# Three more products of the last down projection computed by features: a macaron layer on one core

## The reference

```python
x = x + 0.5 * ffn(layernorm(x))
x = x + scan_mixer(layernorm(x))     # z = x W^T, gated scan over time, layernorm
x = x + 0.5 * ffn(layernorm(x))
# ffn: gate = x Wg^T, up = x Wu^T, hidden = silu(gate) * up, out = hidden Wd^T
```

## Time and profile before

| | us |
|---|---|
| median of 3 runs | 1014.11 (1013.87 to 1014.11) |
| the profiled execution's own time | 1013.8 |
| span of its trace | 1012.0 |
| PE busy | 1005.7 |
| DVE busy | 728.7 |
| ACT busy | 438.2 |
| POOL busy | 202.8 |

### The profile page before, as it was taken

The page is one execution under the profiler, slowest core; times in us unless marked ns, Lnnn a source line. Parts: engine busy times, 40 slices in busy tenths (PEclk is TensorE's granted clock), DMA queues, the critical chain, the costliest instruction groups (busy, mean ns, idle before and its releaser), DMA issues.

```text
span 1012.0 us, 13046 instructions
## 1 busy us (share of the span) xinstructions
PE 1005.7 (99%) x4652; PEld 841.6 (83%) x4652; DVE 728.7 (72%) x1070; ACT 438.2 (43%) x711; POOL 202.8 (20%) x243
## 2 busy tenths in 40 slices
PE   8999999999999999999999999999999999999998
PEld 7888888888888888888888888888888888888897
DVE  7755665598988687857978887786587455654693
ACT  6645446456433623223823344232273434332382
POOL 4123343115400200210421020003040222200032
PEclk9999999999999999999999999999999999999999
DMA  6588877769767545746856764554588799874255
GB/s 208 224 312 332 308 255 255 270 211 277 255 223 239 188 158 165 222 139 227 258 181 211 244 221 148 187 159 147 174 277 261 244 328 332 323 239 167 84 187 187
DMA packets 76319, 228.39 MB, mean 226 GB/s; under 512 B 6624, under 2 KB 26080, under 8 KB 68576
## 3 DMA queue, kind: packets, MB, share of 16 engines
q1 hardware_dynamic: 75680, 226.52, 66.1%
q10 hardware_dynamic: 576, 1.05, 0.3%
HBM read 173.02 MB, written 54.53 MB: 225 GB/s over the span
## 4 chain that ended last, share of the span: by engine, by line
PE 99%; DMA 0%; DVE 0%; POOL 0%; ACT 0%; issue 0%; DVEq 0%; ACTq 0%
PE ps_a L1911 8%; PE ps_a L1910 8%; PE ps_a L1912 8%; PE ps_b L1911 7%; PE ps_b L1910 7%; PE ps_b L1912 7%; PE ps_d L1910 7%; PE ps_d L1911 7%; PE ps_d L1912 7%; PE ps_c L1911 6%; PE ps_c L1910 6%; PE ps_c L1912 6%; PE aux L1911 3%; PE aux L1910 3%; PE aux L1912 3%; PE ps_d L2130 1%
## 5 line engine op out<-in xcount | busy, mean ns | idle before, releaser
L1280 DVE TENSOR_TENSOR tmp<-tmp,ps_c 128x512 f32<-128x512 f32 x59 | 40.4, 685 | 119.2 <-PE ps_c L1912 119.2
L1910 PE MATMUL ps_a<-xt,gu 128*128 128x512 f32 x304 | 118.3, 389 | 0.0
L1911 PE MATMUL ps_a<-xt,gu 128*128 128x512 f32 x304 | 118.3, 389 | 0.0
L1912 PE MATMUL ps_a<-xt,gu 128*128 128x512 f32 x304 | 118.3, 389 | 0.0
L1911 PE MATMUL ps_b<-xt,gu 128*128 128x512 f32 x286 | 111.3, 389 | 0.0
L1912 PE MATMUL ps_b<-xt,gu 128*128 128x512 f32 x286 | 111.3, 389 | 0.0
L1910 PE MATMUL ps_b<-xt,gu 128*128 128x512 f32 x286 | 111.3, 389 | 0.0
L1912 PE MATMUL ps_c<-xt,gu 128*128 128x512 f32 x236 | 91.8, 389 | 0.0
L1911 PE MATMUL ps_c<-xt,gu 128*128 128x512 f32 x236 | 91.8, 389 | 0.0
L1910 PE MATMUL ps_c<-xt,gu 128*128 128x512 f32 x236 | 91.8, 389 | 0.0
L1912 PE MATMUL ps_d<-dn,hid 128*128 128x512 f32 (+1 forms) x224 | 83.7, 374 | 0.0
(11 more groups left out here) (290 smaller groups left out, 2324.8 us busy)
## 6 DMA issues: line engine op xcount, KB each, us to landing
dn<-dn_kept SPq DMA_DIRECT2D x92, 512.0 KB, 4.0
gu<-gu_kept SPq DMA_DIRECT2D x46, 1024.0 KB, 5.1
gu<-gu_kept SPq DMA_DIRECT2D x46, 768.0 KB, 5.6
gu_kept<-gu SPq DMA_DIRECT2D x14, 1024.0 KB, 4.5
gu_kept<-gu SPq DMA_DIRECT2D x14, 768.0 KB, 4.2
dn_kept<-dn SPq DMA_DIRECT2D x16, 512.0 KB, 5.1
t_kept<-zx SPq DMA_DIRECT2D x16, 512.0 KB, 4.7
dn<-t_kept SPq DMA_DIRECT2D x16, 512.0 KB, 3.9
```

The lines of the kernel that those rows point to most:

```text
L1280: dve.tensor_tensor(dst, u3s(si), p5_bank(si)[:, :], ALU.add).then_inc(c22_done, 1)
L1910: pe.matmul(dst, a_hi, b_hi, start=start, stop=False, skip_group_check=chained)
L1911: pe.matmul(dst, a_hi, b_lo, start=False, stop=False, skip_group_check=chained)
L1912: return pe.matmul(dst, a_lo, b_hi, start=False, stop=stop, skip_group_check=chained)
```

## The change

P1, Q6 and Q7 go by features too, so only Q4 stays by tokens. The chain in `x_ps` is now copied by ACT after P1 (for result 0), after Q6 (for result 2) and after Q7 (for result 1), and PE waits for these copies (`feature_copied` 2, 4, 6), where it waited for `block_added`. DVE adds P2 to result 0 and Q5 + Q3 to result 2 in feature form (`add_feature`), and for result 1, which is now twice as large (4 rows instead of 2), it adds the two rows of `x_ps` to the two of `z_ps` (`add_third_link`). Q4 gets four banks of its own, one for each unit of tokens, and DVE adds each unit as it is done (`add_unit`). The quadrant copies of result 0 on ACT move from before batch 10's cast to behind batch 14's. The diff, without the semaphores' declarations:

```diff
@@ -64,8 +64,7 @@
               + [(w, i) for w in (Q7, Q3, Q4) for i in range(4)])
-    ENDED = (Q6, Q7, Q4)
-    PLACED_BY_ACT = 8
+    PLACED_BY_ACT = (8, 10, 8)
     assert tokens == 512 and D == 512 and DT == ST == 4 and HT == 16 and tiles == 4 and K == 4
...
@@ -152,6 +151,7 @@
+        q4_ps = [ps_d[2], ps_d[3], ps_b, ps_c]
...
         def by_tile(ps):
...
@@ -270,17 +270,17 @@
         def feature_rows(job):
-            return (zx_rows[:, 0:2, :], gu_rows[:, 0:2, :], gu_rows[:, 6:8, :])[job]
+            return (zx_rows[:, 0:2, :], gu_rows[:, 0:4, :], zx_rows[:, 6:8, :])[job]
         def turned_rows(job):
-            return (zx_rows[:, 2:4, :], gu_rows[:, 2:4, :], gu_rows[:, 8:10, :])[job]
+            return (zx_rows[:, 2:4, :], gu_rows[:, 4:8, :], zx_rows[:, 0:2, :])[job]
         def token_rows(job):
-            rows = (zx_rows[:, 4:6, :], gu_rows[:, 4:6, :], gu_rows[:, 10:12, :])[job]
+            rows = (zx_rows[:, 4:6, :], gu_rows[:, 8:12, :], zx_rows[:, 2:4, :])[job]
...
         def result_rows(job):
-            return (x_tok[:, 8:12, 0:HALF], x_tok[:, 12:16, HALF:D], x_tok[:, 8:12, HALF:D])[job]
+            return (x_tok[:, 8:12, 0:HALF], x_tok[:, 12:16, :], x_tok[:, 8:12, HALF:D])[job]
         def from_feature(job, q):
...
@@ -705,12 +706,11 @@
-            sp.wait_ge(block_added, 6)
-            store_half(3, 1)
-            sp.wait_ge(result_added, 3)
-            store_half(2, 1)
+            for job in (1, 2):
+                sp.wait_ge(result_added, job + 1)
+                store_half(4 - job, 1)
...
-                sp.wait_ge(block_added, 7 + b)
+                sp.wait_ge(unit_added, 2 * b + 2)
...
@@ -958,19 +958,21 @@
-            def copy_feature(job, banks, semaphore, n):
+            def copy_feature(job, row, banks, semaphore, n):
...
+                if job == 2:
+                    act.wait_ge(t_stored, 32 * PAIRS)
...
-                    act.copy(feature_rows(job)[:, b, :], banks[b][:, :]).then_inc(feature_copied, 1)
+                    act.copy(feature_rows(job)[:, row + b, :], banks[b][:, :]).then_inc(feature_copied, 1)
             def place_feature(job):
-                act.wait_ge(feature_turned, 2 * job + 2)
+                act.wait_ge(feature_turned, (2, 6, 8)[job])
...
-                for q in range(PLACED_BY_ACT):
+                for q in range(PLACED_BY_ACT[job]):
...
             def load_silu():
...
@@ -1093,17 +1095,20 @@
                     hi0(g, 1)
-                    for n in range(1, 20):
+                    stage_hi_of(1)
+                    stage_hi_of(2)
+                    copy_feature(0, 0, x_ps, first_done, 2 * PAIRS - 1)
+                    for n in range(3, 20):
+                        if n == 13:
+                            copy_feature(2, 0, x_ps, batch_done, ENDING.index((Q6, 3)) + 1)
+                        if n == 14:
+                            copy_feature(1, 2, z_ps, batch_done, ENDING.index((Q5, 3)) + 1)
+                        if n == 18:
+                            copy_feature(1, 0, x_ps, batch_done, ENDING.index((Q7, 3)) + 1)
                         stage_hi_of(n)
-                        if n == 4:
-                            copy_feature(0, y_ps, first_done, 2 * PAIRS)
-                        if n == 10:
+                        if n == 14:
                             place_feature(0)
-                        if n == 13:
-                            copy_feature(1, z_ps, batch_done, ENDING.index((Q5, 3)) + 1)
-                        if n == 16:
-                            place_feature(1)
-                    copy_feature(2, z_ps, batch_done, ENDING.index((Q3, 3)) + 1)
+                    place_feature(1)
                     place_feature(2)
...
@@ -1259,8 +1264,8 @@
-                pool.wait_ge(feature_turned, 2 * job + 2)
-                for q in range(PLACED_BY_ACT, 16):
+                pool.wait_ge(feature_turned, (2, 6, 8)[job])
+                for q in range(PLACED_BY_ACT[job], 16):
...
@@ -1414,37 +1419,43 @@
-            def add_block(banks, b, tile, half, semaphore, n, added=0):
+            def add_feature(job, banks, semaphore, n):
...
-                wait(dve, block_added, added)
-                x = x_tok[:, 4 * tile + 2 * b:4 * tile + 2 * b + 2, half * HALF:(half + 1) * HALF]
-                dve.scalar_tensor_tensor(x, by_half(banks[b][:, :]), 0.5, x, ALU.mult, ALU.add
-                                         ).then_inc(block_added, 1)
-            def add_product(w):
-                tile, half, added = {Q6: (2, 1, 0), Q7: (3, 1, 0), Q4: (3, 0, 0)}[w]
-                if w == Q7:
-                    dve.wait_ge(result_added, 2)
-                add_block(x_ps, 0, tile, half, bank_done, ENDED.index(w) + 1, added)
-                add_block(x_ps, 1, tile, half, batch_done, ENDING.index((w, 3)) + 1, added)
+                dve.wait_ge(feature_copied, {0: 2, 2: 4}[job])
+                for b in range(2):
+                    row = feature_rows(job)[:, b, :]
+                    dve.tensor_tensor(row, row, banks[b][:, :], ALU.add).then_inc(feature_added, 1)
+            def add_third_link():
+                dve.wait_ge(feature_copied, 8)
+                rows = feature_rows(1)
+                dve.tensor_tensor(rows[:, 2:4, :], rows[:, 2:4, :], rows[:, 0:2, :], ALU.add).then_inc(feature_added, 1)
             def turn_feature(job):
-                dve.wait_ge(feature_copied, 2 * job + 2)
+                dve.wait_ge(feature_added, (2, 3, 5)[job])
...
-                for r in range(2):
+                if job == 2:
+                    dve.wait_ge(result_added, 1)
+                for r in range((2, 4, 2)[job]):
...
             def add_result(job):
-                dve.wait_ge(act_placed, PLACED_BY_ACT * (job + 1))
-                dve.wait_ge(pool_placed, (16 - PLACED_BY_ACT) * (job + 1))
-                dve.wait_ge(block_added, (2, 4, 6)[job])
+                dve.wait_ge(act_placed, sum(PLACED_BY_ACT[:job + 1]))
+                dve.wait_ge(pool_placed, sum(16 - n for n in PLACED_BY_ACT[:job + 1]))
...
+            def add_unit(t):
+                dve.wait_ge(unit_done, t + 1)
+                dve.wait_ge(result_added, 2)
+                x = x_tok[:, 12 + t, 0:HALF]
+                dve.scalar_tensor_tensor(x, q4_ps[t][:, 0:HALF], 0.5, x, ALU.mult, ALU.add).then_inc(unit_added, 1)
             def zw_lo_of(j):
...
@@ -1870,8 +1881,6 @@
-            for b in range(2):
-                add_block(x_ps, b, 2, 0, first_done, 2 * PAIRS - 1)
...
@@ -1881,27 +1890,26 @@
             stage_lo_of(7)
+            add_feature(0, y_ps, first_done, 2 * PAIRS)
+            stage_lo_of(8)
             turn_feature(0)
-            stage_lo_of(8)
-            add_product(Q6)
             stage_lo_of(9)
...
             stage_lo_of(10)
-            stage_lo_of(11)
+            for n in range(11, 17):
+                stage_lo_of(n)
             add_result(0)
-            stage_lo_of(12)
-            stage_lo_of(13)
+            stage_lo_of(17)
+            add_third_link()
             turn_feature(1)
-            for n in range(14, 17):
-                stage_lo_of(n)
-            add_result(1)
-            stage_lo_of(17)
-            add_product(Q7)
             stage_lo_of(18)
             stage_lo_of(19)
+            add_feature(2, z_ps, batch_done, ENDING.index((Q3, 3)) + 1)
             turn_feature(2)
+            add_result(1)
             add_result(2)
-            add_product(Q4)
+            for t in range(ST):
+                add_unit(t)
...
         def _(pe):
...
@@ -2071,17 +2076,10 @@
                     pe.wait_ge(c12_done, upto(SETS * LAST + 1))
-                if odd:
-                    for b in range(2):
-                        a = slice(b * P, (b + 1) * P)
-                        last = three(y_ps[b][:, :], dn[:, n % DN, 1, 0, a], dn[:, n % DN, 1, 1, a],
-                                     hid0[:, 1, 0, :], hid0[:, 1, 1, :], q == 0, q == PAIRS - 1, True)
-                else:
-                    for t in range(ST):
-                        a = slice(t * P, (t + 1) * P)
-                        last = three(unit_half(x_ps, t), hid0[:, 0, 0, a], hid0[:, 0, 1, a],
-                                     dn[:, n % DN, 0, 0, :], dn[:, n % DN, 0, 1, :], q == 0 and t % 2 == 0,
-                                     q == PAIRS - 1, True)
+                for b in range(2):
+                    a = slice(b * P, (b + 1) * P)
+                    last = three((y_ps if odd else x_ps)[b][:, :], dn[:, n % DN, odd, 0, a], dn[:, n % DN, odd, 1, a],
+                                 hid0[:, odd, 0, :], hid0[:, odd, 1, :], q == 0, q == PAIRS - 1, True)
                 last.then_inc(first_done, 1)
             def batch(m):
...
@@ -2092,27 +2090,33 @@
                     pe.wait_ge(c11_done, upto(SETS * PH - 1))
-                if i == 0 and w == Q3:
-                    pe.wait_ge(feature_copied, 4)
-                if i == 0 and w in (Q6, Q7, Q4):
```

(45 more changed lines are left out.)

## The result

The changed kernel took 1016.77 us (median of 9 runs, 1015.10 to 1018.06), the kernel before 1014.11 (9 runs, 1013.87 to 1014.52): a ratio of 1.0021, interval 1.0012 to 1.0030. It is slower by 2.7 us in the medians, just above what a measurement of this kernel can tell from no change. The median says less than the single runs do: four lie between 1015.10 and 1015.46, four between 1016.77 and 1016.92, and one at 1018.06. The first four have a mean granted clock of 1.000, the others of 0.998 or 0.997.

A forecast was written before the change was run, and what follows sets the result against it. PE was taken to bound the kernel, busy 1005.7 of 1012.0 us. -1.91 (PE's matmuls) + 3.2 (stall at Q7) - 0.27 (last addition) = +1.0 us on 1014.11, so 1015.1 us; range 1013.8 to 1017.0.

The forecast's parts named there:

- likeliest case: Whole kernel: PE stalls at Q7 with its clock staying full, 1015.1 us (own range 1014.5 to 1015.7); chance 0.53.
- slower (over 1016.1): Whole kernel: outcome class of a time over 1016.1 us; chance 0.32.
- What PE saves: PE's matmuls in Q6, Q7, the batch behind changed form, and P1's blocks: 1.91 us less.
- The stall at Q7: PE before Q7 waits for ACT's copies, held behind two casts and DVE's `s4_of`: 3.2 us, bounds 2.7 and 3.7.
- Nothing else waits: PE after Q7: no second wait at Q3 or Q4; `add_result(2)` ends 0.4 us before Q4's first unit is done.
- The last addition: Tail behind PE: DVE's last addition is 128x256 instead of 128x512, 0.42 us for 0.69, so 0.27 us less.
- The clock: Rival: the rest at Q7 drops PE's clock to 1.2 GHz, 1.4 to 1.7 us more, 1016.5 to 1016.8; chance 0.27.
- stall with full clock: At Q7: PE rests about 3.2 us and its clock stays full, 1014.5 to 1015.7 us; chance 0.53.
- stall with the clock down: At Q7: PE rests and its clock falls, 1016.5 to 1016.8 us; chance 0.27.
- The case without a stall: Rival: Q7 starts on time, so only the savings count, 1011.9 us; chance 0.10 for no or a small stall.

The follow-up runs named there:

- the copies ahead: Changed kernel with ACT's two copies of `x_ps` after Q6 moved ahead of the casts of batches 11 and 12: 1011.73 us, ratio 0.9977.
- the second one: Profile of the changed kernel run once more, unedited, on the same chip as its variants: 1016.21 us, ratio 1.0016.
- the shorter rest: Changed kernel with DVE's `s4_of` ahead of batch 9's low part instead of behind it: 1013.66 us, ratio 0.9995.
- the longer rest: Changed kernel with ACT's copies of `x_ps` after Q6 one cast further back, behind batch 13's: 1017.80 us, ratio 1.0041.

## Why the prediction came out as it did

The time, 1016.77, lies in the range of 1013.8 to 1017.0, but near its upper end and 1.7 us above the likeliest case's 1015.1. What came is the case "slower (over 1016.1)", to which I gave 0.32, and one of the nine runs, 1018.06, lies outside the range. Point by point:

- *What PE saves*, 1.91 us. Right. Q6 and Q7 take 10.88 instead of 11.51, batch 7 2.72 instead of 2.75. With the copies ahead the first batch starts at 951.54 instead of 952.15, 0.61 us earlier where I had 0.63 for the blocks of P1, and the last matmul starts at 1006.46, 1.93 us before the 1008.39 of the earlier trace rows. In the profile after, the first batch starts only 0.30 earlier, at 951.85. The reason lies at the start of the program: PE's first matmuls on `hid` began 0.35 later in that run (the first two lines below this list), and from them to the first batch it is 942.86 us against 943.51, 0.65 less. The rule of the Trainium skill that I weighed (TensorE: Matmul & The Clock Gate, section "Back-to-back issue gap") is given there for isolated matmuls, and would have made 0.4 us of it, an estimate by that page. This stream, in which each matmul has weights of its own, does not follow it: a pair costs 13 ns more here, not 2.5.
- *The stall at Q7*, 3.2 us with bounds of 2.7 and 3.7. Right in place, cause and size: 3.22 in the profile after and 3.18 in the second one. The times of the chain are 0.2 to 0.35 us later than I had them, which fits the later start of that run: batch 7's low part at 966.15 for 965.8, `s4_of` at 971.95 for 971.7, ACT's cast of batch 11 at 973.73 for 973.5, the copies' end at 976.7 for 976.5. The time at which Q7 could have started, 973.61 for 973.29, is shifted alike, so the difference holds.
- *Nothing else waits*. Right for PE: Q3 and Q4 start at once in every profiled run. The estimate that `add_result(2)` would end with 0.4 us to spare before the first unit was too kind: it started at 1008.85, and held the first unit's addition by 0.1 us, to 1009.99 instead of some 1009.87. The last addition was not held. POOL's eight copies took 5.5 us for my 5.2.
- *The last addition*, 0.27 us less. Right: 0.42 us against 0.69. With the copies ahead, 3.34 us pass from the last matmul's start to the end of the span, against 3.61 before.
- *The clock*. The mechanism was named and priced, 1.4 to 1.7 us, and it measured 1.6 to 1.7; the medians of the two groups lie 1.6 to 1.7 us apart. The price was partly luck: I took half of the rest's 2.8 us, but the clock stayed full through the rest and was down for 3.4 us of work, and half of that was lost. The failing step is the chance. I wrote "stall with full clock 0.53" and "stall with the clock down 0.27", because one row at the end of the program spoke for it, and the sum has the clock's term at nothing. It happened in 11 of 20 runs, so a median should fall in the upper group about as often as in the lower one, and both measured medians did. I also wrote that the trace before has no matmul at the lower clock. Its clock row has none, but at the start of the program the same small matmuls go at little more than half the pace for the first 3 us of PE's work, 7 in a microsecond against 12 later, while the row reads 1.00 in both. That looks like a low stretch that the row does not record, and half of its 3 us, an estimate of 1.5, would have been a price from matmuls (the last two lines below this list). The likeliest case should not have been a single time: the single row was evidence for a kernel with two times, one for each side of the fall.
- *The case without a stall*, 1011.9. The right price for the kernel that did not have the stall: 1011.7 measured, with the copies ahead.

The lines that two of these points rest on: PE's first matmuls on `hid` before and after, and, in the trace before, two microseconds of the small matmuls at the start (length, busy, matmuls in the record, granted clock, the DMA's share and GB/s).

```profile
8.64 1.96 PE L2180 MATMUL ps_d<-ident,hid 128*128 128x128 f32 x16 [1.37 <-ACT hid L834]
8.99 1.97 PE L2184 MATMUL ps_d<-ident,hid 128*128 128x128 f32 x16 [1.52 <-ACT hid L834]
```

```profile
3.57:4.57 1.00, 1.00 (x7) 1.00 1.05 404
5.57:6.57 1.00, 1.00 (x12) 1.00 1.06 394
```

The Trainium skill's rule (TensorE: Matmul & The Clock Gate, section "Part 1: The HAM clock gate (the "warmup" mystery)"), that the throttled clock is the default and activity releases it, agrees with these traces: the clock fell behind a rest and came back at 981.2 with PE at work.

## What to carry to other kernels

When PE's wait is moved from one engine to another, read what stands ahead of the new releaser in that engine's own list, and what those instructions wait for; here two casts that nobody wanted for another 8 us or more held copies that PE wanted at once, and one moved line turned a loss of 2.0 to 2.7 us into a gain of 2.5. Weigh a rest of PE of the lengths seen here to bring the fall, 2.6 us and more, in otherwise unbroken work with the lower clock behind it, 1.6 to 1.7 us here, in a part of the runs, and look at the single runs and their clocks before believing a median. If such a rest can't be removed, small matmuls in most of it are worth a try: with them the changed kernel took 1015.1 instead of 1016.2 or 1016.8, and no run of 11 showed the fall.

## What the runs showed of the hardware

| PE's unbroken idle time in front of Q7 | runs with a lower mean clock | chip |
|---|---|---|
| 1.2 us (after 1.95 us of small matmuls) | 0 of 11 | first |
| 1.7 us (the shorter rest) | 0 of 11 | first |
| 2.6 us (after 0.60 us of small matmuls) | 6 of 11 | second |
| 3.0 and 3.1 us (the changed kernel, twice) | 11 of 20 | second (6 of 11); not on record (5 of 9) |
| 4.0 us (the longer rest) | 5 of 5 | second |

The idle times are those that the profile gives for PE's wait in one run each. For the rows without small matmuls they are 0.16 us shorter than the rests given above, which count from the time at which Q7 could have started, while the last matmul still shows as busy. Between 1.7 and 2.6 us is where the falls begin in this table. But the two rows without a fall come from another chip than the rows with one, and the changed kernel itself wasn't run there. That this chip's clock falls less readily is not excluded.

I had not expected that the clock falls when PE is at work again: in both profiled runs with a fall it was full through the rest and fell near 977.8 and 978.2, with PE back since 976.83 and 977.73. At the end of the program before it fell within the rest. Nor had I expected that a single rest gives three times: full clock, 1.6 us later, and in three runs of all (1018.06, 1018.81, 1018.88) about a microsecond more, at a mean clock of 0.997. What makes the third is open; none of these was profiled. That two matmuls of 128x256 cost about 13 ns more than one of 128x512 held wherever the clock was full: 11.52 us against 10.88 or 10.89 for the same columns.
